# Transformer block on 8 cores: in the first layer norm, each tile's statistics are issued one tile ahead of its normalization

## The reference, cut to what matters

```python
x = L0_attn_x                                  # [16, 2048, 1024] float32
x = x + attention(layernorm(x))                # 16 heads of 64, qkv with LoRA on q and v, then w_proj
x = x + bitlinear_ffn(layernorm(x))            # inner size 4096, weights and activations quantized

def layernorm(x, eps=1e-5):
    m = mean(x, -1); v = var(x, -1)
    return (x - m) / sqrt(v + eps)
```

## Time and profile before

| | us |
|---|---|
| median of the 2 runs shown | 5471.74 |
| the two runs | 5410.46 and 5533.01 |
| the profiled execution | 5381.64 |
| its span, slowest core (core 3) | 5380.1 |
| spans of the 8 cores | 5345.0 to 5380.1 |
| TensorE busy | 3494.8 (65%) |
| ScalarE busy | 1930.3 (36%) |
| VectorE busy | 1714.9 (32%) |

### The profile page before, as it was taken

One profiled execution on the slowest core, in us unless ns is written; L12 is line 12 of the kernel. 1 busy time (PEld: TensorE's weight loads), 2 busy tenths in 40 slices (PEclk: granted clock), 3 DMA queues, 4 the chain that ended last, 5 costly groups with the idle time before them and its releaser, 6 DMA issues.

```text
span 5380.1 us, 50495 instructions; the slowest of 8 cores (5345.0 to 5380.1 us)
## 1 busy us (share of the span) xinstructions
PE 3494.8 (65%) x15494; PEld 1373.8 (26%) x15494; DVE 1714.9 (32%) x3379; ACT 1930.3 (36%) x2456; POOL 248.9 (5%) x325
## 2 busy tenths in 40 slices
PE   0122196488887576868685196488887666868685
PEld 0111142122122233334232142122122233423242
DVE  5665401211112344343432401211112344343432
ACT  1222331277775023131321331277775023131311
POOL 0001010000000100000000010000000100000000
PEclk9999996588887787979797596588887787979797
DMA  6767131000000331514232131000000331514142
GB/s 225 256 257 214 55 34 10 0 4 4 8 4 3 78 122 58 162 59 145 77 127 79 55 34 10 0 4 4 8 4 3 74 114 63 162 49 161 52 152 67
DMA packets 223509, 403.44 MB, mean 75 GB/s; under 512 B 77968, under 2 KB 143696, under 8 KB 221136
## 3 DMA queue, kind: packets, MB, share of 16 engines
q1 hardware_dynamic: 113024, 221.67, 12.9%
q0 software_dynamic: 110224, 178.54, 12.6%
HBM read 370.81 MB, written 41.94 MB: 77 GB/s over the span
## 4 chain that ended last, share of the span: by engine, by line
PE 53%; DMA 17%; DVE 13%; issue 8%; ACT 8%; DVEq 1%; ACTq 0%; SPq 0%; POOLq 0%
PE ps_all L712 9%; PE ps_all L902 8%; PE ps_all L895 8%; PE ps_all L564 7%; PE ps_all L992 6%; PE ps_all L724 5%; DMA dstream<-s_dT 3%; ACT exps L736 3%; PE ps_all L966 3%; DMA x<-x 2%; PE ps_all L762 2%; DMA den_all<-o_tmp 2%; DVE hq L957 2%; DVE o_tmp L681 2%; DMA wp_st<-w_gate 2%
## 5 line engine op out<-in xcount | busy, mean ns | idle before, releaser
L736 ACT ACTIVATE exps<-ps_all 128x1024 bf16<-128x1024 f32 x1024 | 973.6, 1049 | 282.1 <-PE ps_all L730 257.5
L712 PE MATMUL ps_all<-exps,v_tm 128*65 128x512 bf16 x2048 | 728.2, 436 | 222.7 <-DVE o_tmp L681 128.1
L902 PE MATMUL ps_all<-tstream,xi_fm 128*128 128x512 bf16 x2048 | 786.5, 384 | 61.1 <-DMA tstream<-s_uT 61.1
L895 PE MATMUL ps_all<-tstream,xi_fm 128*128 128x512 bf16 x2048 | 787.9, 385 | 0.0
L992 PE MATMUL ps_all<-dstream,hi_fm 128*128 128x512 bf16 x2048 | 468.2, 390 | 33.9 <-DMA dstream<-s_dT 26.1
L730 PE MATMUL ps_all<-q_fm,k_fm 64*128 64x512 bf16 x1024 | 419.3, 429 | 0.0
L912 ACT ACTIVATE silu_t<-ps_all,colb 128x512 f32<-128x512 f32 x256 | 175.9, 687 | 677.1 <-PE ps_all L895 673.9
L724 PE MATMUL ps_all<-q_fm,k_fm 64*128 64x512 bf16 x1024 | 418.7, 429 | 0.0
L966 PE MATMUL ps_all<-eyebf,hq 128*128 128x128 bf16 x1024 | 149.0, 299 | 354.2 <-DVE hq L957 354.2
L916 DVE SCALAR_TENSOR_TENSOR h_sb<-ps_all,colb,silu_t 128x512 bf16<-128x512 f32 x256 | 192.1, 751 | 584.5 <-ACT silu_t L912 463.4
L564 PE MATMUL ps_all<-xn_fm,wst_b 128*128 128x512 bf16 x1536 | 366.5, 404 | 4.8 <-DVE xn_fm L528 4.8
(11 more groups left out here) (106 smaller groups left out, 3126.8 us busy)
## 6 DMA issues: line engine op xcount, KB each, us to landing
tstream<-s_gT SPq DMA_DIRECT2D x64, 1024.0 KB, 5.4
tstream<-s_uT POOLq DMA_DIRECT2D x64, 1024.0 KB, 8.2
wp_st<-w_gate SPq DMA_DIRECT2D x8, 4096.0 KB, 16.2
wp_st<-w_up SPq DMA_DIRECT2D x8, 4096.0 KB, 16.4
wp_st<-w_down SPq DMA_DIRECT2D x8, 4096.0 KB, 14.9
dstream<-s_dT SPq DMA_DIRECT2D x40, 768.0 KB, 4.5
dstream<-s_dT POOLq DMA_DIRECT2D x40, 768.0 KB, 5.1
xstage<-x SPq DMA_DIRECT2D x32, 512.0 KB, 3.7
```

Of the source, the lines that this page charges most:

```text
L712: (lambda l_, r_, po_, st_, sp_: lambda e: e.matmul(PS[0:65, po_, 0:QWS], l_, r_, start=st_, stop=sp_))(v_tm[:, kt, h, 0:65], exps[:, kt % ...
L736: (lambda d_, s_: lambda e: e.activation(d_, s_, AF.Exp, scale=ASCALE))(exps[:, kt % 3, :, :], PS[:, pa:pa + 2, 0:QWS]),
L895: (lambda l_, r_, k_, st_, sp_: lambda e: e.matmul(PS[:, k_, 0:FWS], l_, r_, start=st_, stop=sp_))(xi_fm[:, cc, k * 128:(k + 1) * 128], ts ...
L902: (lambda l_, r_, k_, st_, sp_: lambda e: e.matmul(PS[:, 4 + k_, 0:FWS], l_, r_, start=st_, stop=sp_))(xi_fm[:, cc, k * 128:(k + 1) * 128] ...
```

## The change

`layernorm` is split into `ln_stats` (the Squares and the VectorE operations up to plus eps) and `ln_finish` (Ln, Exp and -mean * rstd). The statistics get a set of columns and a dependency buffer for each parity (`B("lncols", 0)` at columns 0 to 6 and `B("lncols", 1)` at columns 53 to 59 of `colb`), and the normalized tile gets a second buffer, `xn1t2`. The LN1 loop emits the DMA and the statistics of tile `ti + 1` ahead of the Ln, Exp, normalization, transposes and copies of tile `ti`. The two staging buffers of x stay two. `ffn_a_sv` still calls `layernorm`, which is now `ln_stats` followed at once by `ln_finish`.

```diff
+        xn1t2 = sb.at("xn1t2", [128, C], BF16, tr_off + 8 * C)
...
-    def layernorm(src_ap, src_buf, scratch, dbl, scratch_buf=None):
-        ssq = colb[:, 0:1]
...
-        bc = B("lncols")
+    def ln_stats(src_ap, src_buf, scratch, dbl, scratch_buf=None):
+        base = (0, 53)[dbl]
+        ssq = colb[:, base:base + 1]
...
+        bc = B("lncols", dbl)
...
         p.op("vector", lambda e: e.tensor_scalar_add(var, var, 1e-5),
              reads=[bc], writes=[bc])
+
+    def ln_finish(dbl):
...
         p.op("scalar", lambda e: e.activation(var, var, AF.Ln),
              reads=[bc], writes=[bc])
...
+    def layernorm(src_ap, src_buf, scratch, dbl, scratch_buf=None):
+        ln_stats(src_ap, src_buf, scratch, dbl, scratch_buf)
+        return ln_finish(dbl)
...
-        for ti in range(KT):
+        def ln1_a(ti):
             xs = xstage[:, 0, :] if ti % 2 == 0 else xstage2[:]
             bxs = B("xs", ti % 2)
             r0 = s * N + ti * 128
             p.dma("sync", ...
                   writes=[bxs])
-            rstd, nmr, brs = layernorm(xs, bxs, sqs, ti % 2)
-            p.op("scalar", (lambda s_, r_, n_: lambda e: e.activation(
-                xn1t[:], s_, AF.Identity, bias=n_, scale=r_))(xs, rstd, nmr),
-                reads=[bxs, brs, B("xn1t")], writes=[B("xn1t")])
+            ln_stats(xs, bxs, sqs, ti % 2)
+            return xs, bxs
+
+        ln_st = {0: ln1_a(0)}
+        for ti in range(KT):
+            if ti + 1 < KT:
+                ln_st[ti + 1] = ln1_a(ti + 1)
+            xs, bxs = ln_st.pop(ti)
+            rstd, nmr, brs = ln_finish(ti % 2)
+            xnt = xn1t if ti % 2 == 0 else xn1t2
+            bxt = B("xn1t", ti % 2)
+            p.op("scalar", (lambda d_, s_, r_, n_: lambda e: e.activation(
+                d_[:], s_, AF.Identity, bias=n_, scale=r_))(xnt, xs, rstd, nmr),
+                reads=[bxs, brs, bxt], writes=[bxt])
             transpose_tile_to(
-                xn1t, B("xn1t"), CC,
+                xnt, bxt, CC,
```

More of the change, by code:

```diff
@@ L274, in build_program @@
         sqs = sb.alloc("sqs", [128, 512], F32)
+        xn1t2 = sb.alloc("xn1t2", [128, C], BF16)
         wst_f = sb.alloc("wst_f", [128, 2, CC, 128], F32)
@@ L464, in build_program @@
     sb.release()
-    def layernorm(src_ap, src_buf, scratch, dbl, scratch_buf=None):
-        ssq = colb[:, 0:1]
[L468 to L471, removed]
+    def ln_stats(src_ap, src_buf, scratch, dbl, scratch_buf=None):
+        base = (0, 53)[dbl]
+        ssq = colb[:, base:base + 1]
+        ssum = colb[:, base + 1:base + 2]
+        mean = colb[:, base + 2:base + 3]
+        m2 = colb[:, base + 3:base + 4]
+        var = colb[:, base + 4:base + 5]
         rstd = colb[:, 8 + dbl * 2:9 + dbl * 2]
         nmr = colb[:, 9 + dbl * 2:10 + dbl * 2]
-        bc = B("lncols")
+        bc = B("lncols", dbl)
         brs = B("rstd", dbl)
@@ L477, in layernorm @@
         ncq = max(1, C // 512)
+        assert ncq <= 3
         for ci in range(ncq):
             cw = min(512, C)
-            part = ssq if ncq == 1 else colb[:, 6 + ci:7 + ci]
+            part = ssq if ncq == 1 else colb[:, base + 5 + ci:base + 6 + ci]
             p.op("scalar", (lambda s_, o_: lambda e: e.activation(
@@ L485, in layernorm @@
         if ncq == 2:
-            p.op("vector", lambda e: e.tensor_add(ssq, colb[:, 6:7], colb[:, 7:8]),
-                 reads=[bc], writes=[bc])
+            p.op("vector", lambda e: e.tensor_add(
+                ssq, colb[:, base + 5:base + 6], colb[:, base + 6:base + 7]),
+                reads=[bc], writes=[bc])
         elif ncq > 2:
             p.op("vector", (lambda n_: lambda e: e.tensor_reduce(
-                ssq, colb[:, 6:6 + n_], AX.X, ALU.add))(ncq),
+                ssq, colb[:, base + 5:base + 5 + n_], AX.X, ALU.add))(ncq),
                 reads=[bc], writes=[bc])
@@ L503, in layernorm @@
              reads=[bc], writes=[bc])
+    def ln_finish(dbl):
+        base = (0, 53)[dbl]
+        mean = colb[:, base + 2:base + 3]
+        var = colb[:, base + 4:base + 5]
+        rstd = colb[:, 8 + dbl * 2:9 + dbl * 2]
+        nmr = colb[:, 9 + dbl * 2:10 + dbl * 2]
+        bc = B("lncols", dbl)
+        brs = B("rstd", dbl)
         p.op("scalar", lambda e: e.activation(var, var, AF.Ln),
```

## The result

| | before | changed |
|---|---|---|
| median | 5434.81 us (36 runs) | 5434.04 us (37 runs) |
| lowest run | 5376.86 | 5409.72 |
| profiled execution | 5381.64 | 5419.39 |
| spans of the 8 cores | 5345.0 to 5380.1 | 5380.7 to 5417.8 |

The ratio of the changed kernel to the one before is 1.0055, with a 95% interval from 1.0034 to 1.0077: slower by some 30 us (0.0055 * 5381.64), between 18 and 41. In some executions of either kernel one die of the chip is clocked lower and the time is up to 4% longer; the ratio leaves these out, the medians don't, and that is why the medians say nothing here.

The account below looks back on a forecast made before the run. LN1 was taken as bound by an engine-to-engine chain, all exposed; rounds growing from 8.35 to 10.27 us added 52 us to the two-run median 5471.74, giving 5524 us (1.0095), range 5430 to 5585.

Parts of the forecast that it names:

- The chain that was foreseen: LN1 round: normalization's end, x fetch, Squares, statistics, -mean * rstd, next normalization; 10.27 us, 1.92 us above 8.35.
- its two main links: In LN1's round: the x fetch, 3.7 us, and -mean * rstd queued on VectorE behind the next tile's statistics, 2.89 us.
- Rival A: In LN1, the x fetch stays hidden: rounds of 7.8 us, -17 us, 5455 us; chance 6 in 100.
- C: In LN1, only every second fetch is on the path: rounds of 9.0 us, about +17, 5489; chance 8 in 100.
- Rival B: In LN1, each fetch costs 4.7 us: +80 us, 5552; chance 12 in 100, of them 4 past 2%.
- The sum: LN1's first round, 14 middle rounds and last round: +26.7 us in sequence 1, +25.8 in sequence 2, together +52.
- normalization's end to the Square: LN1 round: 0.13 us to the DMA's issue, 3.7 to landing, 0.3 to the Square; 4.13 us.
- to VectorE, statistics: LN1 round: from the Squares' accumulator read to VectorE and through the statistics operations, 2.89 us.
- -mean * rstd: LN1 round: VectorE's column operation next after the statistics, 0.10 us gap plus 0.21, together 0.31 us.
- The ends of the loop: LN1: normalization 0 starts 3.2 and 1.95 us later; the last round takes 5.0 us instead of 8.35.
- The parts at nothing: Split columns, also in the second layer norm, and second buffer xn1t2: forecast to be worth nothing.
- The start of qkv: Behind LN1: longer pauses could cost another slow start, 2.8 us each, at most 5.6; taken as 0.

Follow-up runs that it names:

- e1: Changed kernel with a third staging buffer for x: ratio 0.9976 to the kernel before, LN1 21.4 us shorter than before.
- e3: Changed kernel, two staging buffers, with LN1's -mean * rstd computed on ScalarE: ratio 0.9927 to the kernel before, LN1 32.9 us shorter.
- e7: Changed kernel with each x tile of LN1 fetched twice: first Square to last normalization 200.5 and 203.0 us, from 147.9 and 149.3; no ratio.
- e8: Kernel before with each x tile of LN1 fetched twice: first Square to last normalization 130.8 and 131.8 us, as without it; no ratio.
- e2: Changed kernel without the hoist, keeping split columns and second xn1t: ratio 1.0024 to the kernel before, LN1 131.0 and 131.2 us.
- e6: Changed kernel reordered, two buffers: next tile's statistics and finish between transposes and copies. LN1 56.7 us shorter than before; ratio 0.9896 from a rerun.

## Why the prediction was off in size and right in kind

**The kind.** The chain that was foreseen is the one in the trace, link by link, and each of its two main links was shown by taking it away (e1, e3) and the first by doubling it (e7, e8). Rivals A and C would have needed Squares that don't wait; all 32 wait. Rival B would have needed fetches of 4.7 us; the median is 3.5. The kernel became slower, by less than 2%.

**The base.** The forecast of 5524 was 5471.74, the median of two runs, plus 52. With 36 runs the median of the same kernel is 5434.81, so 37 of the 90 us between 5524 and 5434.04 lie in the base. The other 53 are the 52 us of the forecast change and the 0.8 us by which the two medians differ the other way; the medians show nothing of the change, and its size is to be had from the ratio and the profiles. The prediction had noted that the two runs stood 2.3% apart and that the profiled one lay 90 us under their median, and built on the median all the same. This step, adding to 5471.74, failed. Like against like, the profiled executions are 5381.64 and 5419.39, 37.8 us apart, and the lowest runs 5376.86 and 5409.72, 32.9 apart.

**The sum.** +52 us was forecast (1.0095) and 34.6 came in LN1 (1.0055 in the whole, and 1.0095 is outside the interval). The step that failed is the length of a round, 10.27 us against 9.56 and 9.66 in the mean of the two sequences, with the chain right and some of its terms too long. Its terms, from the round shown above:

| term | forecast | measured | from |
|---|---|---|---|
| normalization's end to the Square | 4.13 | 3.67 | 563.40 to 567.07 |
| two Squares | 1.54 | 1.53 | to 568.60 |
| to VectorE, statistics | 2.89 | 2.69 | to 571.29 |
| -mean * rstd | 0.31 | 0.17 | to 571.46 |
| to the normalization and through it | 1.40 | 1.39 | to 572.85 |
| round | 10.27 | 9.45 | |

Three terms were too large. For the fetch the prediction took a median of 3.7 from one core of the kernel before, where the 8 cores have medians of 3.4 to 3.7, and 0.3 us from landing to Square. In the round above x is issued at 563.53 and lands 3.4 us later, 0.14 us ahead of the Square; at the first tile of the same trace (530.45, and 3.6 us) it is 0.29. That 0.3, and the 0.3 from ScalarE to VectorE, were read at the first tile of a sequence, since nowhere else in the kernel before did a Square wait for x. The changed kernel has both cases of the second one in one trace too, the first tile and the second of sequence 1:

```profile
535.69 0.19 ACT L485 ACTIVATION_READ_ACCUMULATOR sqs<-xstage 128x1 f32 x1
536.18 0.16 DVE L490 TENSOR_TENSOR colb<-colb 128x1 f32<-128x1 f32 x1 [16.39 <-ACT sqs L485]
...
540.06 0.19 ACT L485 ACTIVATION_READ_ACCUMULATOR sqs<-xstage 128x1 f32 x1
540.35 0.16 DVE L490 TENSOR_TENSOR colb<-colb 128x1 f32<-128x1 f32 x1 [1.56 <-ACT colb L518]
```

0.30 us from the end of the accumulator read to VectorE in the first tile, 0.10 in the second, and 0.10 in the round above. By the program the first instruction of an engine behind a fence has more semaphores to wait for, and VectorE had also been idle for longer (16.39 us against 1.56); which of the two makes the difference is not shown. For -mean * rstd the prediction took the usual pause between small operations of one chain; the instruction ahead of it belongs to the other tile, and it starts 0.11 us behind that one's start, with no pause (571.14 and 571.25). Together these are 0.82 us in the round shown; the mean round was 0.71 us shorter than forecast in sequence 1 and 0.61 in sequence 2: times 14 each, 18.5 us. The ends of the loop were right or near: counted from the first Square, normalization 0 came 3.4 us later than before (forecast 3.2) and in sequence 2 some 2.3 (1.95), the last rounds took 5.00 and 4.98 (5.0). So 52.5 - 18.5 + 0.6 = 34.6, as measured.

**The parts at nothing.** The split columns, `xn1t2` and the second layer norm: e2 shows no effect in LN1, and none that can be measured in the whole. The start of qkv was put at 0 as well. The granted clock in LN1 of sequence 2 is 0.50 as before, and in sequence 1 the first 12 us of qkv have the 16 and 30 matmuls of the earlier trace rows:

```profile
687.35:693.35 6.00, 6.00 (x16) 2.23 (x16) 0.00 (x0) 0.00 (x0) 0.00 (x0) 1.00 0.01 3
693.35:699.35 6.00, 6.00 (x30) 2.70 (x29) 0.00 (x0) 2.71 (x4) 0.88 (x1) 1.00 0.03 3
```

In sequence 2 they are 45 in the first 12 us, and 43 before. So the start of qkv cost nothing more.

**Rival A's price** was right too, as far as it can be checked: 7.8 us a round and -17 us were worked out for a fetch that is hidden; with the third buffer it was 7.5 to 7.6 us and -21.4.

The Trainium skill (Trainium Kernel Development and Optimization, Best Practices) says to double-buffer so that DMA and compute overlap. This case's traces agree for the kernel before and show what the sentence leaves to the reader: two buffers overlap a fetch with one round's work only if a tile's first reader comes after the last reader of the tile before (e6: two buffers, no wait); when the first reader is hoisted ahead of that, it takes three (e1).

## What to carry to other kernels

Before work is hoisted one iteration ahead, count the buffers that it reads: a stage that runs one tile earlier needs one more buffer for its input, or its fetch, hidden until then, lands on the path (+34.6 us here against -21.4 with the buffer). Another order can spare the buffer (e6). And don't price a wait by its length: of the 3.7 us only the 2.0 counted in which no other work of the chain was done. Then look at what stands behind the hoisted work in each in-order queue: one column operation behind the next tile's statistics was worth as much as the fetch, and putting it on the engine that reads it took the time to 0.9927 of the kernel before with two buffers and to 0.9821 with three. Take hand-over times from the steady state, not from the first instruction behind a fence, and add the sum to the profiled execution, from which its terms come, rather than to a median of two runs that lie 2.3% apart.

## What the runs showed of the hardware beside this

Two small VectorE operations of 0.15 to 0.21 us start 0.26 to 0.32 us apart when the second needs the result of the first (570.29, 570.55, 570.87 and 571.14 in the round of the changed kernel), and 0.11 us apart when it belongs to another chain (571.14 and 571.25). By this, chains of single-column operations of two tiles, interleaved, might take less of VectorE than one behind the other; this wasn't tried. A fetch of 512 KB took 3.3 to 5.0 us on this core with all eight cores fetching at the same time, and issuing each twice, the second behind the first as the program orders it, cost 3.5 us more each time (e7).
